# First attention of a two-layer mixer: where the folding of the experts' first two matrices stands

## The reference, cut to what matters

```
h = einsum('td,edh->teh', x, w1) + b1
gated = silu(einsum('teh,ehf->tef', h, wg) + bg) * (einsum('teh,ehf->tef', h, wv) + bv)
y = einsum('tef,efd->ted', gated, w2) + b2
```

## Time and profile before

| what | us |
|---|---|
| median of three runs (2272.18 to 2274.57) | 2273.43 |
| the profiled execution, its own time | 2275.42 |
| its span, first to last instruction | 2273.5 |
| one body of an image in the middle, 461.21 to 569.14 | 107.93 |
| TensorE busy over the span | 1929.1 (85%) |
| VectorE busy over the span | 1436.2 (63%) |
| ScalarE busy over the span | 1098.7 (48%) |

### The profile page before, as it was taken

One profiled execution on the slowest core, in us unless ns is written; L12 is line 12 of the kernel. 1 busy time (PEld: TensorE's weight loads), 2 busy tenths in 40 slices (PEclk: granted clock), 3 DMA queues, 4 the chain that ended last, 5 costly groups with the idle time before them and its releaser, 6 DMA issues. The chain is left out here.

```text
span 2273.5 us, 41046 instructions
## 1 busy us (share of the span) xinstructions
PE 1929.1 (85%) x13306; PEld 1073.3 (47%) x13307; DVE 1436.2 (63%) x3154; ACT 1098.7 (48%) x1682; POOL 755.4 (33%) x883
## 2 busy tenths in 40 slices
PE   5769999999999999998589996996659992699993
PEld 2331223332332323232367774554447661599992
DVE  4769888888888888871346665762235665344444
ACT  4550665666666666666144442541225551344442
POOL 0232003343333333345335553000001667355551
PEclk9875999999999999999699998999879996799995
DMA  3851532323232323012333333322100242233326
GB/s 127 193 217 33 78 55 29 60 35 65 31 66 29 66 29 66 2 38 63 105 86 99 95 99 119 111 84 61 38 29 29 62 136 81 71 94 92 90 72 229
DMA packets 134782, 180.00 MB, mean 79 GB/s; under 512 B 44592, under 2 KB 87856, under 8 KB 132336
## 3 DMA queue, kind: packets, MB, share of 16 engines
q1 hardware_dynamic: 116208, 138.25, 25.6%
q0 software_dynamic: 18432, 39.88, 5.2%
HBM read 99.04 MB, written 69.01 MB: 74 GB/s over the span
## 5 line engine op out<-in xcount | busy, mean ns | idle before, releaser
L779 DVE TENSOR_REDUCE mx<-bank 128x1 f32<-128x512 f32 x1024 | 639.7, 696 | 86.4 <-PE bank L550 85.2
L726 ACT ACTIVATE P<-bank 128x1024 f32<-128x1024 f32 x512 | 497.4, 1021 | 313.1 <-PE bank L652 312.9
L550 PE MATMUL bank<-ks,qs 96*128 96x512 bf16 x1024 | 358.6, 402 | 35.5 <-DVE mx L779 35.5
L1290 POOL DMA_INDIRECT results<-yo,places x284 | 274.1, 965 | 283.6 <-DVE yo L1280 236.8
L652 PE MATMUL bank<-qs,ks 99*128 99x512 bf16 x1024 | 308.2, 384 | 2.6 <-ACT P L726 1.8
L1206 PE MATMUL bank<-xt,up 128*128 128x256 f32 x1136 | 274.8, 386 | 3.7 <-DVE xt L1257 1.4
L632 PE MATMUL bank<-P,vt 128*32 128x512 f32 x2048 | 272.8, 605 | 0.7 <-ACT P L726 0.7
L2289 POOL DMA_INDIRECT dispatched<-planes,places x128 | 124.5, 973 | 420.2 <-DVE stats L2133 357.3
L1206 PEld LDWEIGHTS bank<-xt,up 128*128 128x128 f32 x1136 | 207.5, 193 | 30.4 <-issue 4.7
L550 PEld LDWEIGHTS bank<-ks,qs 96*128 96x128 bf16 x1024 | 99.8, 98 | 257.5 <-DVE mx L779 177.7
L652 PEld LDWEIGHTS bank<-qs,ks 99*128 99x128 bf16 x1024 | 78.0, 97 | 280.0 <-ACT P L726 182.8
(11 more groups left out here) (298 smaller groups left out, 2581.8 us busy)
## 6 DMA issues: line engine op xcount, KB each, us to landing
xr<-dispatched SPq DMA_DIRECT2D x142, 130.0 KB
qk_parts<-parts SPq DMA_DIRECT2D x16, 768.0 KB, 5.1
qs<-qk_parts SPq DMA_DIRECT2D x84, 128.0 KB
ks<-qk_parts SPq DMA_DIRECT2D x84, 128.0 KB
v_turned<-vt SPq DMA_DIRECT2D x8, 1024.0 KB, 5.6
vt<-v_turned SPq DMA_DIRECT2D x8, 1024.0 KB
bands<-results SPq DMA_DIRECT2D x32, 256.0 KB, 3.7
y<-results SPq DMA_DIRECT2D x32, 256.0 KB
```

Source lines behind the costliest of these rows:

```text
L550: pe.matmul(bank[:, slot, :], qs[par][0:KB, h, c * C:(c + 1) * C], ks[par][0:KB, h, half * HALF:(half + 1) * HALF], start=True, stop=True) ...
L726: act.activation(P[:, x % SLOTS, :], bank[:, 2 * pair:2 * pair + 2, :] .rearrange("p a t -> p (a t)"), ACT.Exp).then_inc(probs_ready, 1)
L779: dve.tensor_reduce(mx[:, k // 2, k % 2:k % 2 + 1], bank[:, slot, :], AX.X, ALU.max).then_inc(unit_freed, 1)
L1290: pool.indirect_dma_start(yd_dram, bass.IndirectOffsetOnAxis(places[:, p, q:q + 1], 0), yo[:, p, q, :], None).then_inc(sent[p], 16)
```

## The change

The folding leaves the end of the stage. It becomes three kinds of units, `fold_turn`, `fold` and `fold_bias`, in the bodies of images 1 to 7. The body of image b folds expert b - 1, at steps 20, 22 and 24; the last body folds expert 6 at steps 10, 12 and 14 and expert 7 at steps 20, 22 and 24. The three use the units' banks and semaphores, and VectorE evicts them in place of ScalarE: a copy of 128x256, a copy of 128x512 and an addition of 128x4. SP loads an expert's matrices after the unit `proj 1` of the body (a 128 KB transfer of w1 into the place of the result and one of 513 KB into a buffer of its own, `source`). At the end SP's queue holds only the blanks. The list of units is longer, so the other units also shift by a step here and there.

```diff
+    for step, k in ((11, 0), (21, 1)):
+        for n, kind in enumerate(("fold_turn", "fold", "fold_bias")):
+            at = (step + 2 * n) * len(units) // STEPS
+            units.insert(at, (kind, k))
     return units
...
+def expert_of(before, k):
+
+    return before + k if before == B - 2 else before
...
+            and not (unit[0] in FOLDS and unit[1] == 0 and more)]
...
+            def load_source(e, unit, base, units):
+                sp.wait_ge(unit_filled, base + units.index(unit) + 1)
+                sp.dma_start(wres[:, e, 0:2 * C], to_fold[e, :, 0:W1_COLS]).then_inc(source_loaded, 16)
+                sp.dma_start(source[:], to_fold[e, :, W1_COLS:W1_COLS + WGV_COLS + 2]).then_inc(source_loaded, 16)
...
+                if prev:
+                    load_source(b - 1, ("proj", 1), base, units)
                 max_rows(b, par, 1)
...
-            load_source(4)
-            load_source(5)
-            send_blanks(1)
-            load_source(6)
-            load_source(7)
-            send_blanks(2)
-            send_blanks(3)
+            for part in range(4):
+                send_blanks(part)
...
+            def multiply(e, slot, turned):
+                pe.wait_ge(unit_freed, turned)
                 for k in range(2):
...
+                    ins = pe.matmul(bank[:, slot, :], wres[:, e, (4 + k) * C:(5 + k) * C], source[:, k * 4 * C:(k + 1) * 4 * C],
...
-                turn_w1(0)
-                turn_w1(1)
-                multiply(0)
-                sum_bias(0)
                 for n in range(2):
                     project(B - 1, n, 5 + n)
...
-                for e in range(2, E):
-                    if e + 1 < E:
-                        turn_w1(e + 1)
-                    multiply(e)
-                    sum_bias(e)
...
+            def copy_product(e, slot, filled):
+                dve.wait_ge(unit_filled, filled)
+                dve.tensor_copy(wres[:, e, 0:4 * C], bank[:, slot, :]).then_inc(unit_freed, 1)
```

More of the change, by code:

```diff
@@ L347, in units_of @@
 def units_of(prev, more):
-    return [unit for unit in BODY_UNITS if (more or not of_next(unit)) and (prev or unit[0] in ("max", "rows"))]
+    return [unit for unit in BODY_UNITS if (more or not of_next(unit)) and (prev or unit[0] in ("max", "rows"))
+            and not (unit[0] in FOLDS and unit[1] == 0 and more)]
 FIRST_UNITS = [unit for unit in units_of(False, True) if of_next(unit)]
@@ L398, in attend_and_route_first @@
     ex, un = sb("ex", [C, TILES], F32), sb("un", [C, TILES], F32)
[L400 to L406, removed]
+    flat_P = P[:].rearrange("c s n -> c (s n)")
+    source = sb("source", [C, WGV_COLS + 2], F32)
+    passed = flat_P[:, 0:TILES * E].rearrange("c (n e) -> c n e", e=E)
+    skip = flat_P[:, TILES * E:2 * TILES * E].rearrange("c (n e) -> c n e", e=E)
+    past = flat_P[:, 2 * TILES * E:2 * TILES * E + TOKENS // SLOT * E].rearrange("c (e n) -> c e n", e=E)
     count = ends
     blank = a[:].rearrange("c g t -> c (g t)")[:, 0:E // 2 * SQ * ROW].rearrange("c (n r) -> c n r", n=E // 2)
-    source_loaded = [sem("source0_loaded"), sem("source1_loaded")]
-    w1_turned, w1_copied, multiplied = sem("w1_turned"), sem("w1_copied"), sem("multiplied")
-    product_copied, bias_summed, bias_loaded, bias_added = sem("product_copied"), sem("bias_summed"), sem("bias_loaded"), sem("bias_added")
+    source_loaded, bias_loaded = sem("source_loaded"), sem("bias_loaded")
     centred_router, router_ready, routing_set = sem("centred_router"), sem("router_ready"), sem("routing_set")
@@ L506, in body @@
                     load_v(b + 1, 1 - par)
+                units, base = units_of(prev, more), units_before(b) if prev else len(FIRST_UNITS)
+                if prev:
+                    load_source(b - 1, ("proj", 1), base, units)
                 max_rows(b, par, 1)
@@ L519, in _ @@
             body(B - 1, 1, True, False, False)
[L520 to L521 removed]
+            last_units = units_of(True, False)
+            load_source(E - 1, ("fold_bias", 0), units_before(B - 1), last_units)
+            sp.wait_ge(unit_filled, units_before(B - 1) + last_units.index(("fold_bias", 1)) + 1)
             for e in range(E):
@@ L667, in body @@
                                 logits(before, slot)
+                            elif kind == "fold_turn":
+                                turn_w1(expert_of(before, k), slot)
+                            elif kind == "fold":
+                                multiply(expert_of(before, k), slot, base + units.index(("fold_turn", k)) + 1)
+                            elif kind == "fold_bias":
+                                sum_bias(expert_of(before, k), slot)
                             else:
@@ L761, in last @@
                 reciprocal(B - 1, 3)
-                copy_w1(0)
-                copy_w1(1)
-                copy_product(0)
                 rstds(B - 1)
                 exponentials(B - 1)
-                for e in range(1, E):
-                    if e + 1 < E:
-                        copy_w1(e + 1)
-                    copy_product(e)
-                act.wait_ge(product_copied, E)
             over_images(act, first, body, last)
@@ L821, in copy_ranks, with copy_w1, add_bias @@
                 dve.tensor_copy(flat(ranked), bank[:, slot, 0:(G + 1) * E]).then_inc(unit_freed, 1)
+            def copy_w1(e, slot, filled):
+                dve.wait_ge(unit_filled, filled)
+                dve.tensor_copy(wres[:, e, 4 * C:6 * C], bank[:, slot, 0:2 * C]).then_inc(unit_freed, 1)
+            def copy_product(e, slot, filled):
+                dve.wait_ge(unit_filled, filled)
+                dve.tensor_copy(wres[:, e, 0:4 * C], bank[:, slot, :]).then_inc(unit_freed, 1)
+            def add_bias(e, slot, filled):
+                dve.wait_ge(unit_filled, filled)
+                dve.wait_ge(bias_loaded, 16)
+                dve.tensor_tensor(biases[:, e, :], bank[:, slot, 0:4], biases[:, e, :], ALU.add).then_inc(unit_freed, 1)
             def weigh_experts(then, b, copied):
@@ L903, in body @@
                             copy_logits(before, slot, filled)
+                        elif kind == "fold_turn":
+                            copy_w1(expert_of(before, k), slot, filled)
+                        elif kind == "fold":
+                            copy_product(expert_of(before, k), slot, filled)
+                        elif kind == "fold_bias":
+                            add_bias(expert_of(before, k), slot, filled)
                         else:
@@ L976, in last @@
                     blank_part(part)
-                dve.wait_ge(bias_loaded, 16)
-                dve.wait_ge(bias_summed, E)
-                flat_biases = biases[:].rearrange("c e k -> c (e k)")
-                dve.tensor_tensor(flat_biases, bank[:, BIAS_BANK, 0:4 * E], flat_biases, ALU.add).then_inc(bias_added, 1)
-                dve.wait_ge(bias_added, 1)
                 dve.wait_ge(unit_freed, LAST + 6)
```

51 lines of the change are left out of this document (10 added, 41 removed).

## The result

The changed kernel took 2299.82 us (median of four runs, 2296.39 to 2305.29); the kernel before, on the same chip, 2272.8. The ratio is 1.012, with a 95% interval of 1.0095 to 1.0144: slower by 27 us, where 11.4 were forecast. The profiled execution took 2296.39, with a span of 2294.5.

The account below looks back on a forecast made before the run. TensorE and VectorE were taken to hold each other in the bodies, SP's order to space the blanks at the end. Six bodies 25.2 plus last body 6.2 less end 20 gave +11.4 us, 2284.8 us; 8-in-10 range 2268 to 2295.

Parts of the forecast that it names:

- The end: End of the stage: SP sends blanks when filled, they and POOL's scatter meet at 1121 against 1141.75; gain taken as 20 us.
- the case without a source in flight: Blanks at the stage's end: a landing takes 2.5 us, against up to 5.5 to 6.4 beside a source load.
- I take nothing: Image 7's projection at the end: a later clock rise could give back up to 4 us; counted as nothing.
- TensorE's price in the bodies: Bodies: one expert costs TensorE 3.8 us at full clock (transposes 0.25, multiplication 1.72, bias 1.84), paid in full.
- the low end's argument: Bodies: each of three folding units uses up one 0.21 us wait and the spread costs nothing; 3.2 us a body, 19 in all.
- The spread: Bodies: the unit list spread anew, steps 12 and 14 holding three units and others five; 0.4 us a body.
- I take 4.2 us a body: Folding's whole cost in each of six bodies, 25.2 us together; range 19 to 32.
- the rest of the last body: Last body folds experts 6 and 7, 7.6 us of TensorE; cost taken as 6.2 us, between 3 and 8.
- +11.4: Whole kernel: forecast net slowdown in us, 25.2 for six bodies plus 6.2 for the last less 20 at the end.
- hidden in the bodies: Rival: folding fits into room in the bodies, a third of its price (10 us) left; faster, 2263 us; chance 0.12.
- the end did shorten: Denies the rival that the end hardly shortens: scatter slows the blanks, gain only 10 us; +21, 2295 us; chance 0.12.

Follow-up runs that it names:

- the run without folding: The change with matrix multiplication, loads, matmuls and evictions of the folding left out, units at their old steps: 2250.86 us, ratio 0.9893.
- that with four buffers: Kernel before, folding still at the end, four source buffers in place of two, loads of experts 4 and 5 ahead of the blanks: 2253.70 us, ratio 0.991.
- the shifted steps alone: Kernel before, its bodies' units spread as in the change, with holes where the folding's units would stand: 2279.10 us, ratio 1.0032.
- the wide bias: The change with each bias-sum matmul 128 columns wide in place of one, so the result is not the biases; the text gives no time.
- no bias sum: The change without the unit `fold_bias`, so the biases stay unfolded: 2284.13 us, ratio 1.0062.
- the old steps and folding: The change, older units at their previous steps, three runs: folding at 21, 23, 25, 2287.89 us; bias matmuls 128 wide besides, 2283.03; folding at 20, 22, 24, 2283.69.
- the longer wait: Kernel before with two 128x512 fills added on VectorE between step 18's operations that choose the best expert: 2283.73 us, ratio 1.0055.

## Why the prediction was wrong

**The end: right.** Forecast 20 us, measured 21.2. SP sends each part when it is filled, and POOL's scatter and the last blanks end the stage together. VectorE's waits between the fills (5.43 and 6.30 us) are mostly the sending: the last transfers of the second and the third part are issued at 1150.2 and 1158.2, and the next fills begin at 1152.91 and 1160.42, so they land within 2.7 and 2.2 us, as in the earlier trace rows and not as in the earlier trace rows. That is what was taken for the case without a source in flight. "I take nothing" for the clock of the projection held: its second half runs at full clock (1.02 us at 1121.30).

**TensorE's price in the bodies: right in kind, its size tied to the steps around it.** In a body without a fall, steps 22 and 24 last 4.58 and 4.48 us (image 1, by the starts of the product with the values), as forecast, and no room was found in them. With the older units at their old steps the folding costs 3.17 us, not 3.8. That the low end's argument (each of the three units uses up one wait of 0.21: 3.17) gives the same is luck: the transposes' step is 0.33 longer than before, the multiplication's 1.72 and the bias sum's 1.22, so that nearly all is saved in one step. On the shifted steps, which the change has, the folding costs 4.33. At the odd steps it is 3.73.

**The spread: mis-sized.** "Twice 0.26 lost, less some slack: 0.4." The shifted units alone cost 0.56 us. With the folding on them the sum is 4.9 an undisturbed body, 0.7 above "I take 4.2 us a body": 4.2 us over six bodies. In the rest of the last body it was 7.3 in place of 6.2.

**The step that failed** is the unspoken one in the same sum: that TensorE's clock stays full in the bodies, because the earlier trace rows show 1.00 there. In the changed kernel 27.3 us of the bodies run at half clock (added up over cuts of 1 us), and the five bodies with falls are together 9.8 us longer than five times the 112.82 of the one without. With 4.2 for the mis-sized bodies, 1.1 for the last, 1.3 ahead of them and -1.2 for the end, these 9.8 make up, but for rounding, the 15.1 us between +11.4 and +26.5. The prediction weighed the clock only where TensorE idles, at the end, and there it cost nothing. So its price of one expert "at full clock" lacked a term of 1.6 us a body in this profile, and this term alone is larger than the mis-sized ones together.

**What sets the falls off** is shown in part. At step 18 TensorE has a thin place: the wait of 1.45 us stands in the kernel before as well, as this row of its timeline shows,

```profile
493.93 0.39 PE L550 MATMUL bank<-ks,qs 96*128 96x512 bf16 x1 [1.45 <-DVE mx L779]
```

and in 18 bodies (images 1 to 6 of the kernel before, of the run without folding and of that with four buffers) no fall follows it. With the fifth unit in that step, which splits the work after the wait by another 0.21 us, falls follow in 16 of 30 bodies (the change twice, the shifted steps alone, the wide bias, no bias sum); with that one unit moved away in 0 of 6; with the old steps and folding in 3 of 18. Behind the narrow bias matmuls they follow in 11 of 30 bodies, behind wide ones in none of 12. So both places are real, and the longer wait shows that step 18 needs no folding for it. That the moved unit and the wide matmuls remove falls is what the counts say, not more: the moved unit rests on one profile of six bodies, in which the falls behind step 24 are missing too, without an edit there. Nor are narrow matmuls enough by themselves, as the kernel before has the sixteen of `logits` in each of its bodies from image 1 to 7, and no fall behind them. Open stays why the same rows bring a fall in one body and none in the next. The Trainium skill ("TensorE: Matmul & The Clock Gate", section "A second HAM failure mode: psum-queue depth-cycling") tells of a kernel that cycles through PSUM banks, in which short idle times between groups of matmuls let the clock swing between its two levels. The traces agree in kind for step 18, where TensorE waits 1.45 us for one of three banks, and add a place whose records show no wait at all: the sixteen instructions from 524.05 to 525.92.

**The rivals.** Nothing was hidden in the bodies, and the end did shorten; the time went out of the range (2268 to 2295) because of a case that was not among them. Less the 9.8 us of the falls, the account's +26.5 is +16.7: inside the range, whose upper end is +21.6, but still above the forecast. The run with one unit moved, whose profile has no falls, is 20.8 us slower than before, just inside.

## What to carry over

The folding's own work did not make the stage end late; the order of its loads and the blanks on one queue, with two buffers, did. Before moving work from a place where it seems to wait into one where it costs its full price, look at what is issued behind it: two more buffers and another order on one queue gave nearly the whole gain of the end (20 of 21 us) and left the bodies alone. And where a loop keeps TensorE just full, price an added unit by a test of the fullest step and of the one with the longest wait: a full granted clock before is no promise of one after. The places to look at first are a further stop in a step that already waits, and a run of one-column matmuls in the loop.

## What the runs showed of the hardware

TensorE's clock fell to its lower level in a loop in which TensorE is busy 95% of the time (107.68 of 112.82 us in a body without a fall), in some bodies after a wait as short as 1.45 us, in some after sixteen fp32 instructions of one column that the records count as 1.95 us of work without a gap. Scores then take 1.03 us a pair in place of 0.60. A fall of 3.4 us cost 1.3 to 1.7 us between bodies otherwise alike (112.82 and 114.11; 108.49 and 109.97; 111.73 and 113.41), and which bodies are hit differs from profile to profile of the same kernel. The price of a folding also depends on its place: the same three units cost 3.17 us a body at steps 20, 22, 24 and 3.73 one step later, with the other units where they were.
